# Last layer of a four-layer convolution kernel: loads and stores cut into parts, and border transfers issued by ScalarE instead of SyncE

## The chip, the cores and the metric

The program runs on one core of one Trainium2 chip. The metric is the device time of one execution, in microseconds (us). The core has five engines that run beside each other, each through its own list of instructions in order: TensorE (PE in the profile, its weight loads PEld), VectorE (DVE), ScalarE (ACT), GpSimd (POOL) and SyncE (SP). They meet only at semaphores. DMA transfers are issued by an engine's instruction list and then run beside it; SP and ACT have a queue of their own each.

## The reference

Four layers, each of which adds a residual. Only the last is touched by the change. Its core, on x of 4 images x 48 channels x 256 x 256 in float32:

```
x = x + _L3_conv_ref(_gn(x), w_in, w_dw, fft_mask, w_out)

y = jnp.einsum('oc,bchw->bohw', w_in, x)                  # 48 -> 288 channels
f = jnp.fft.rfft2(yp) * fft_mask[None]                    # on patches of 8 x 8
yp = jnp.fft.irfft2(f, s=(P, P))
y = lax.conv_general_dilated(y, w_dw, (1, 1), ((1, 1), (1, 1)), feature_group_count=C2)   # 3 x 3, each channel alone
x1, x2 = jnp.split(y, 2, axis=1)
g = jax.nn.gelu(x1, approximate=False) * x2
return jnp.einsum('oc,bchw->bohw', w_out, g)              # 144 -> 48 channels
```

## The kernel before

The last layer is `stage_l3`. It is unrolled: 66 **slabs**, n = 0 to 65. A slab is a band of 8 image rows (33 bands, of which the last only closes the image) of two images at once; patches are 8 x 8 = 64 pixels, 32 patches to a band. The filter with the mask and the 3 x 3 convolution are folded into one matrix for each channel, `d` (64 x 100: a patch of 8 x 8 in, 10 x 10 out). The ring of one pixel around each patch belongs to its neighbours and has to be added there: left and right by a transfer from partition to partition (`edge`), below through a saved strip (`strip`).

What PE does in a slab, in this order (`slab` at L2348; the line of the matmul in brackets):

- `convolve(n, 0)` (L2298): 5 groups of channels from `y` and `d` into PSUM banks
- `transpose(n-1, 2)` (L2320): the gated result of the slab before, channel block 2, turned
- `convolve(n, 1)` (L2298), then `project(n-1)` (L2334), the last matmul of the slab before
- `transpose(n, 0)` (L2320), which waits for both halves of the gated block 0 of this slab
- `convolve(n, 2)` (L2298)
- `channels(n+1)` (L2255): the 1 x 1 matmul of the next slab, in 12 groups, from `x` to PSUM
- `transpose(n, 1)` (L2320)

Each convolved **block** (j = 0, 1, 2; u = 3n + j counts all of them) goes the same way. ACT copies one half of each PSUM bank pair to `turn` (L2389, called from `read_turn`) and DVE the other (L2383). When both are through (`a_out`, `b_out`), POOL sets a border to zero (L2523, it then signals `parted`), and two DMAs carry the outer columns of `turn` to `edge`, one for each side (L2203, in `move_edges`; 126 partitions of 1920 bytes). The second waits for `parted`. POOL then zeroes the ends of `edge` (L2526), adds `edge` (L2528), adds `strip` (L2534, in every band but the first; it signals `carried`) and saves the new strip (L2538, it signals `saved`, without which the next block's L2523 doesn't start). ACT computes the Gelu of two halves (L2396, it waits for `carried`), DVE multiplies each half with its gate (L2472), PE transposes, and ACT copies the turned banks to `rows` (`read_rows`, L2389). After `project`, DVE adds the residual in four pieces m (L2480, `f_out`), and the slab is stored.

What sets the order of the transfers is SP's list (`slab` at L2226), which holds every transfer of the layer. For slab n:

- `load_x(n+1)` when `channels(n)` has read the last of `x` (there is one `x` buffer): for each of two images 48 partitions x 8 KB in one DMA (L2187), and a row of ones on one partition (L2189)
- `move_edges(n, 0)` and `move_edges(n, 1)`
- `store(n-1)`: two DMAs of 384 KB (L2209), when all four pieces of the result are there
- `move_edges(n, 2)`
- `load_residual(n)`: four DMAs of 192 KB (L2218), when the store has landed

ACT's own list before the change (`slab` at L2411): the five copies of block 0 with the two Gelu halves of the slab before between them; four `read_rows` copies of `transpose(n-1, 2)`; the five copies of block 1; the two Gelu halves of block 0; four `read_rows` copies; the five copies of block 2; then the 12 copies of `channels(n+1)` (`read_y`) with the two Gelu halves of block 1 between them; and four `read_rows` copies. `conv_at(n, j, g)` is the count at which group g of block j of slab n begins in `a_done` (PE has written) and `a_out` (ACT has read).

Of the kernel before, what the change touches and what calls it, by code (L numbers as in the profile page):

```python
# [16 lines left out]
B, C, H, W = 4, 48, 256, 256  # L17
# [5 lines left out]
HI = 64  # L23
# [2072 lines left out]
def stage_l3(nc, D, S):  # L2096

    C3 = 3 * C
    TX, PX = W // 8, 64
    BANDS = H // 8 + 1  # L2100
    N = 2 * BANDS
# [9 lines left out]
    LANE = 32  # L2111
    GROUPS = PX // 4
    with nc.cleanup_on_exit(), ExitStack() as ctx:
        def sb(name, shape):
# [5 lines left out]
        def sem(name):  # L2120
            return nc.alloc_semaphore(f"l3_{name}")
# [20 lines left out]
        d_in = [sem(f"d_in{j}") for j in range(3)]  # L2142
        x_loaded, res_loaded, stored = sem("x_loaded"), sem("res_loaded"), sem("stored")
        edge_in = [sem("edge_in0"), sem("edge_in1")]
# [7 lines left out]
        def conv_at(n, j, g):  # L2152

            return n * AB + YR + j * COMP + g
# [21 lines left out]
        def _(sp):  # L2176
            for dst, src in ((win, "l3_win"), (wout[:], "l3_wout")):
                sp.dma_start(dst, D[src]).then_inc(consts, 16)

            def load_x(q, ty, n, first):  # L2180
                if not first:
                    sp.wait_ge(a_done, n * AB - (AB - YR))
                    sp.wait_ge(b_done, n * AB - (AB - YR))
                for s in range(2):
                    at = B * NBLK if ty == BANDS - 1 else ty + (q + 2 * s) * NBLK
                    src = D["x3p"][bass.ds(at + 2, 1)]
                    sp.dma_start(x[s * HI:s * HI + C].rearrange("p t x -> p (t x)"), src.rearrange("a c n -> (a c) n"))\  # L2187
                      .then_inc(x_loaded, 16)
                    sp.dma_start(x[s * HI + C:s * HI + C + 1].rearrange("p t x -> p (t x)"), D["k_ones3"][bass.ds(ty, 1), :])\  # L2189
                      .then_inc(x_loaded, 16)  # L2190

            def move_edges(n, j):

                u = n * 3 + j
                sp.wait_ge(a_out, conv_at(n, j, COMP))
                sp.wait_ge(b_out, conv_at(n, j, COMP))
                if u >= 2:
                    sp.wait_ge(edged, u - 1)
                here, there = slice(0, 126), slice(2, 128)
                for side, column, dst, src in ((0, 9, there, here), (1, 0, here, there)):  # L2200
                    if side == 1:
                        sp.wait_ge(parted, u + 1)
                    sp.dma_start(edge[dst, u % 2, side, :],  # L2203
                                 turn[src, u % 2, column].rearrange("p y g i -> p (y g i)")).then_inc(edge_in[u % 2], 16)

            def store(n):
                sp.wait_ge(f_out, n * 4 + 4)
# [4 lines left out]
            def load_residual(q, ty, n, first):  # L2212
                if not first:
                    sp.wait_ge(stored, n * 32)
                for s in range(2):
                    for side in range(2):
                        src = D["x3"][q + 2 * s, :, ty * 8 + 4 * side:ty * 8 + 4 * side + 4, 1:W + 1]
                        sp.dma_start(out[side * HI:side * HI + C, :, s, :], src).then_inc(res_loaded, 16)  # L2218
            load_x(0, 0, 0, True)
            for j in range(3):  # L2220
# [15 lines left out]
            store(N - 1)  # L2236
            sp.wait_ge(stored, N * 32)

        @block.tensor
        def _(pe):  # L2240
            def channels(q, n, first):

                pe.wait_ge(x_loaded, n * 64 + 64)
                for g, size in enumerate(SIZES):
# [142 lines left out]
        def _(act):  # L2387
# [3 lines left out]
            def gelu(u, h):  # L2391
# [198 lines left out]
```

## Time and profile before

| | us |
|---|---|
| median of 3 runs | 12194.6 (12163.93 to 12206.02) |
| the profiled execution | 12186.19 |
| its span on the core | 12184.1 |
| of it the last layer, about | 9442 to 12153 |

The page of the profile gives the busy time of each engine, a strip of 40 slices of the span, the queues of the DMA engines, and the groups of instructions with what ended the idle time before them. The releaser "issue" stands for time in which an engine waited for nothing that the profile shows. The rows are taken from one execution. In the rows names of buffers stand without their prefix and number: l_x is `x`, l_turn is `turn`, l_a, l_b and l_e are the PSUM banks. q1 is SP's queue, q8 and q14 are queues of kind "instruction".

### The profile page before, as it was taken

What the parts mean: (1) busy time and instruction counts of PE and PEld (TensorE: products, weight loads), DVE (VectorE), ACT (ScalarE), POOL (GpSimd) and SP (SyncE); (2) the same over time, 40 slices, a digit from 0 to 9 for tenths busy, and PEclk for the clock granted to TensorE, in tenths of its full rate; (3) what the DMA queues carried; (4) which work ended last, traced back from release to release, by engine and by line L of the source; (5) the groups of instructions that cost most, each with busy time, mean ns of one, the idle gap of its engine ahead of it and who ended that gap; (6) DMA issues with size and microseconds to landing.
All of it is one profiled execution on the core that took longest, in us unless ns stands there. A gap on an engine that the chain in (4) does not pass through costs nothing. (4 is left out here: it accounts for less than half of the span.)

```text
span 12184.1 us, 377334 instructions
## 1 busy us (share of the span) xinstructions
PE 11485.7 (94%) x157286; PEld 8059.9 (66%) x157286; DVE 7073.4 (58%) x16108; ACT 5169.6 (42%) x10670; POOL 4924.0 (40%) x4166
## 2 busy tenths in 40 slices
PE   8999999899979999899999999999999888888888
PEld 7877444399977777555555555555555777777776
DVE  0000355544435544688888888888887665566655
ACT  0000111143433333355555555555554666666666
POOL 0000222211430045566666666666665444444444
PEclk9999999999989999899999999999999999999999
DMA  4333466695894489766666666666665443344433
GB/s 141 132 131 133 126 159 157 151 169 102 149 169 150 135 211 231 115 88 88 88 88 89 88 88 89 88 88 88 88 88 78 109 101 92 92 100 96 99 91 91
DMA packets 2340706, 1418.36 MB, mean 116 GB/s; under 512 B 1877404, under 2 KB 2250395, under 8 KB 2253487
## 3 DMA queue, kind: packets, MB, share of 16 engines
q1 hardware_dynamic: 2064428, 1296.69, 53.7%
q10 hardware_dynamic: 275072, 105.14, 3.7%
q8 instruction: 812, 13.30, 0.5%
q14 instruction: 394, 3.23, 0.1%
HBM read 648.90 MB, written 450.45 MB: 90 GB/s over the span
## 5 line engine op out<-in xcount | busy, mean ns | idle before, releaser
L1795 PE MATMUL l_m<-l_wa,l_pix 128*128 128x288 f32 x8192 | 2210.6, 413 | 2.7 <-DVE l_wb L1977 2.7
L1795 PEld LDWEIGHTS l_m<-l_wa,l_pix 128*128 128x128 f32 x8192 | 1475.1, 190 | 688.4 <-issue 361.5
L1651 POOL TENSOR_TENSOR l_qkv<-l_qkv,l_copies 128x576 f32<-128x576 f32 x1024 | 1437.0, 1403 | 629.2 <-DVE l_qkv L1988 618.4
L1641 POOL TENSOR_TENSOR l_pix<-l_raw 128x516 f32<-128x516 f32 x1024 | 1217.1, 1189 | 1043.5 <-DVE l_t L2025 1018.2
L1476 PE MATMUL l1h_ps<-l1h_ring,l1h_w 96*96 96x256 f32 x6120 | 1327.2, 379 | 63.6 <-ACT l1h_ring L1418 60.0
L1476 PEld LDWEIGHTS l1h_ps<-l1h_ring,l1h_w 96*96 96x96 f32 x6120 | 999.1, 163 | 391.6 <-issue 60.2
L1509 DVE SCALAR_TENSOR_TENSOR l1h_ring<-l1h_ps,l1h_bias,l1h_columns 96x256 f32<-96x256 f32 x1020 | 671.1, 658 | 677.3 <-PE l1h_ps L1476 671.6
L509 PE MATMUL l0a_rows<-l0a_x 128*49 128x245 f32 x8144 | 1043.8, 371 | 0.0
L870 PE MATMUL l0b_bank<-l0b_x,l0b_w 49*64 49x512 f32 x9216 | 1001.1, 593 | 4.4 <-DVE l0b_w L896 4.4
L1890 ACT ACTIVATE l_ks<-l_f 94x384 f32<-94x384 f32 x1024 | 498.7, 487 | 838.6 <-PE l_f L1810 838.6
L1810 PE MATMUL l_f<-l_qkv,l_a 64*94 64x384 f32 x4096 | 835.0, 483 | 1.6 <-POOL l_qkv L1651 1.5
L870 PEld LDWEIGHTS l0b_bank<-l0b_x,l0b_w 49*64 49x64 f32 x9216 | 438.8, 133 | 563.9 <-issue 563.9
L1801 PE MATMUL l_m<-l_wb,l_left 58*128 58x288 f32 x4096 | 773.9, 455 | 0.0
L1460 POOL TENSOR_TENSOR l1h_columns<-l1h_blocks,l1h_ring 96x2048 f32<-96x2048 f32 x63 | 351.0, 5595 | 1035.0 <-DVE l1h_ring L1509 1035.0
L1901 ACT ACTIVATE l_y<-l_i,l_shift,l_rsd 128x96 f32<-128x96 f32 x2048 | 711.2, 428 | 14.3 <-DVE l_shift L2015 0.6
L1895 ACT ACTIVATE l_sd<-l_mv,l_eps 128x4 f32<-128x4 f32 x512 | 152.2, 297 | 1288.0 <-DVE l_mv L2008 1288.0
L1224 PE MATMUL l1v_ps<-l1v_ring_w,l1v_w 48*48 48x130 f32 x20480 | 633.3, 273 | 45.9 <-ACT l1v_ring_w L1147 39.1
L509 PEld LDWEIGHTS l0a_rows<-l0a_x 128*49 128x49 f32 x8144 | 601.4, 124 | 107.7 <-issue 1.4
L2383 DVE COPY l_turn<-l_b 128x500 f32<-128x500 f32 (+1 forms) x528 | 351.6, 666 | 471.8 <-PE l_b L2298 471.5
L2298 PE MATMUL l_e<-l_d,l_y 64*64 64x100 f32 x17424 | 497.0, 255 | 134.5 <-issue 128.4
L1224 PE MATMUL l1v_ps<-l1v_ring_p,l1v_w 48*48 48x128 f32 x20320 | 616.0, 269 | 5.3 <-issue 4.9
L1224 PEld LDWEIGHTS l1v_ps<-l1v_ring_w,l1v_w 48*48 48x48 f32 x20480 | 588.0, 120 | 49.0 <-issue 48.8
(272 smaller groups left out, 22221.3 us busy)
## 6 DMA issues: line engine op xcount, KB each, us to landing
l0a_x<-x_px_dram SPq DMA_DIRECT2D x128, 1176.0 KB, 5.1
l_edge<-l_turn SPq DMA_DIRECT2D x396, 236.2 KB
l0b_x<-x_in_dram SPq DMA_DIRECT2D x128, 493.8 KB
l_raw<-l_raw SPq DMA_DIRECT2D x128, 483.6 KB, 7.3
l_raw<-x_dram SPq DMA_DIRECT2D x1270, 48.0 KB, 3.6
l_x<-x3p_dram SPq DMA_DIRECT2D x132, 384.0 KB
l_out<-x_dram SPq DMA_DIRECT2D x264, 192.0 KB, 4.4
out_dram<-l_out SPq DMA_DIRECT2D x132, 384.0 KB, 4.5
```

What stands on the lines that cost most here:

```text
L509: last = nc.tensor.matmul(o[odd * ODD:odd * ODD + C1, lo:lo + n * C1], x[:, ks, ys, 2 + odd, :], x[:, k, y, e0 + odd:e0 + odd + n, :].rear ...
L870: last = nc.tensor.matmul(bank[2 * n + rt][h * HI:(h + 1) * HI, :], w[part, t, :], rows(part, k, 4 * n + h + t // 3 - rt)[:, :, t % 3:t % ...
L1224: last = nc.tensor.matmul(ps[g][side(c), r, 0:width], w[side(r), t, :], x, start=(t == 0), stop=(t == TAPS - 1), skip_group_check=True)
L1476: last = nc.tensor.matmul(ps[g][0:C2, 0:GI * V], w[:, kernel, s, :], ring[:, g, before % DEEP, :, s:s + V], start=(s == 0), stop=(s == 2))
L1509: nc.vector.scalar_tensor_tensor(out=ring[:, g, x % DEEP, :, 1:V + 1], in0=ps[g][0:C2, 0:GI * V].rearrange("p (i v) -> p i v", i=GI), scal ...
L1641: nc.gpsimd.tensor_tensor(pix[:, n % 2, i, half * HALF:(half + 1) * HALF].rearrange("p (r w) -> p r w", w=PW), in0, in1, op).then_inc(pix_ ...
L1651: nc.gpsimd.tensor_tensor(q, q, copies[:, g % 2, 1:2, :].broadcast_to([128, 2, OUTC]), ALU.add)\
L1795: last = nc.tensor.matmul(bank[i][:, 0:OUTC], pix[:, k, i, first:first + 128], wa[:, b, i, :], start=True, stop=(i in (1, 2)))
L1801: nc.tensor.matmul(bank[i][:, 0:OUTC], left[rows, k, first:first + 128], wb[rows, b, :], start=False, stop=True).then_inc(conv_done, 1)
L1810: last = nc.tensor.matmul(f[0:SLOTS, h, 0:2 * QK].rearrange("p (n o) -> p n o", n=2), a[k, 0:SLOTS], qkv[k, j % 4, 2 * r:2 * r + 2, 0:QK], ...
L1890: nc.scalar.activation(ks[:, r % 2], f[0:SLOTS, :, 0:2 * QK].rearrange("p h (n o) -> p h n o", n=2)[:, :, :, C2:QK], ACT.Copy).then_inc(k_ ...
L1901: last = nc.scalar.activation(y[:, g, m, :], iv[:, m * C2:(m + 1) * C2], ACT.Identity, scale=rsd[:, g, m:m + 1], bias=shift[:, g, m:m + 1])
```

## The change

All in `stage_l3`:

- **x** is loaded in four parts of 8 patches for each image (48 x 2 KB, 96 KB): the first when `channels(n)` is through, the others behind group 2 of `convolve(n, 0)` and groups 0 and 2 of `convolve(n, 1)`. The row of ones is loaded for 4 of the 66 slabs only (where its content changes).
- **The store** is cut into the four pieces m for each of two sides (96 KB), each when DVE has added its residual and PE has come to group m of `convolve(n, 2)`.
- **The residual load** keeps its four DMAs; they are spread over groups 2, 5, 8 and 11 of `channels(n+1)`.
- **The border transfers** leave SP. ACT issues them on its own queue, each pair behind ACT's last copy of the block, with the same waits.

```diff
-            def load_x(q, ty, n, first):
-                if not first:
-                    sp.wait_ge(a_done, n * AB - (AB - YR))
-                    sp.wait_ge(b_done, n * AB - (AB - YR))
+            def load_x(n, k):
+
+                ty, q = n % BANDS, n // BANDS
+                tiles = slice(k * TX // PARTS, (k + 1) * TX // PARTS)
                 for s in range(2):
                     at = B * NBLK if ty == BANDS - 1 else ty + (q + 2 * s) * NBLK
-                    src = D["x3p"][bass.ds(at + 2, 1)]
-                    sp.dma_start(x[s * HI:s * HI + C].rearrange("p t x -> p (t x)"), src.rearrange("a c n -> (a c) n"))\
-                      .then_inc(x_loaded, 16)
+                    src = D["x3p"][at + 2].rearrange("c (t x) -> c t x", x=PX)
+                    sp.dma_start(x[s * HI:s * HI + C, tiles], src[:, tiles]).then_inc(x_loaded, 16)
...
+            def store(n, m):
+                sp.wait_ge(f_out, n * 4 + m + 1)
                 for side in range(2):
-                    sp.dma_start(D["out"][n, side], out[side * HI:side * HI + C].rearrange("p y s w -> p (y s w)"))\
-                      .then_inc(stored, 16)
...
+                    sp.dma_start(D["out"][n, side].rearrange("c (y n) -> c y n", y=4)[:, m],
+                                 out[side * HI:side * HI + C, m].rearrange("p s w -> p (s w)")).then_inc(stored, 16)
...
             def slab(q, ty, n, first, last):
                 if not last:
-                    load_x(*((1, 0) if q == 0 and ty == BANDS - 1 else (q, ty + 1)), n + 1, False)
-                move_edges(n, 0)
-                move_edges(n, 1)
+                    sp.wait_ge(a_done, n * AB + YR)
+                    sp.wait_ge(b_done, n * AB + YR)
+                    if n + 1 in ONES:
+                        load_ones(n + 1)
+                    load_x(n + 1, 0)
+                    sp.wait_ge(a_done, conv_at(n, 0, 3))
+                    load_x(n + 1, 1)
+                if not last:
+                    for k in range(2, PARTS):
+                        sp.wait_ge(a_done, conv_at(n, 1, 2 * k - 3))
+                        load_x(n + 1, k)
+                for m in range(4):
+                    if not first:
+                        if m > 0:
+                            sp.wait_ge(a_done, conv_at(n, 2, m))
+                        store(n - 1, m)
                 if not first:
-                    store(n - 1)
-                move_edges(n, 2)
-                load_residual(q, ty, n, first)
+                    sp.wait_ge(stored, n * 128)
+                for k in range(4):
+                    if not last:
+                        sp.wait_ge(a_done, (n + 1) * AB + 3 * k + 2)
+                    load_residual(q, ty, k // 2, k % 2)
...
+            def move_edges(n, j):
+
+                u = n * 3 + j
+                act.wait_ge(a_out, conv_at(n, j, COMP))
+                act.wait_ge(b_out, conv_at(n, j, COMP))
+                if u >= 2:
+                    act.wait_ge(edged, u - 1)
+                here, there = slice(0, 126), slice(2, 128)
+                for side, column, dst, src in ((0, 9, there, here), (1, 0, here, there)):
+                    if side == 1:
+                        act.wait_ge(parted, u + 1)
+                    nc.scalar.dma_start(edge[dst, u % 2, side, :],
+                                 turn[src, u % 2, column].rearrange("p y g i -> p (y g i)")).then_inc(edge_in[u % 2], 16)
...
                     read_turn(act, copy, 0, n, 0, g, a_done, a_out)
                     if g in (0, 2) and not first:
                         gelu(u - 1, g // 2)
+                move_edges(n, 0)
                 if not first:
                     read_rows(n - 1, 2)
                 for g in range(COMP):
                     read_turn(act, copy, 0, n, 1, g, a_done, a_out)
+                move_edges(n, 1)
                 for h in range(2):
                     gelu(u, h)
                 read_rows(n, 0)
                 for g in range(COMP):
                     read_turn(act, copy, 0, n, 2, g, a_done, a_out)
+                move_edges(n, 2)
```

On ACT, from the last copy of block 0 to the Gelu of block 0. Before:

```order
L2389 ACTIVATE l_turn<-l_e 128x100x4
L2389 ACTIVATE l_rows<-l_a 128x512
L2389 ACTIVATE l_rows<-l_b 128x512
L2389 ACTIVATE l_rows<-l_e 128x512 x2
L2389 ACTIVATE l_turn<-l_a 128x100x5
L2389 ACTIVATE l_turn<-l_e 128x100x5
L2389 ACTIVATE l_turn<-l_a 128x100x5 x2
L2389 ACTIVATE l_turn<-l_a 128x100x4
L2396 ACTIVATE l_turn<-l_turn 128x8x4x24 x2
```

and in the changed kernel, in which L2397 is the copy, L2404 the Gelu and L2417 the border transfer:

```order
L2397 ACTIVATE l_turn<-l_e 128x100x4
L2417 DMA l_edge<-l_turn 126x480 x2
L2397 ACTIVATE l_rows<-l_a 128x512
L2397 ACTIVATE l_rows<-l_b 128x512
L2397 ACTIVATE l_rows<-l_e 128x512 x2
L2397 ACTIVATE l_turn<-l_a 128x100x5
L2397 ACTIVATE l_turn<-l_e 128x100x5
L2397 ACTIVATE l_turn<-l_a 128x100x5 x2
L2397 ACTIVATE l_turn<-l_a 128x100x4
L2417 DMA l_edge<-l_turn 126x480 x2
L2404 ACTIVATE l_turn<-l_turn 128x8x4x24 x2
```

The pair of block 0 now stands ahead of the four copies to `rows`, and the pair of block 1 ahead of the Gelu of block 0.

On SP, one slab before (l_x from x3p is the load of x, l_out from x_dram the residual, out_dram the store):

```order
L2187 DMA l_x<-x3p_dram 48x2048
L2189 DMA l_x<-k_ones_dram 1x2048
L2203 DMA l_edge<-l_turn 126x480 x4
L2209 DMA out_dram<-l_out 48x2048 x2
L2203 DMA l_edge<-l_turn 126x480 x2
L2218 DMA l_out<-x_dram 48x4x256 x4
```

(the first two rows stand there twice in turn), and in the changed kernel:

```order
L2189 DMA l_x<-x3p_dram 48x512 x8
L2201 DMA out_dram<-l_out 48x512 x8
L2207 DMA l_out<-x_dram 48x4x256 x4
```

The border transfers and, in most slabs, the ones are gone from SP's list; x and the store go out in eight DMAs each.

## Rows read from the trace of the kernel before

**Rows 1.** The page, queues of the DMA engines: packets, MB, share of 16 engines.

```profile
q8 instruction: 812, 13.30, 0.5%
```

**Rows 2.** Busy by stretch: PE, PEld, DVE, ACT, POOL, clock, DMA share, GB/s.

```profile
9442.00:12153.00 2711.00, 2323.68 (x64288) 1948.03 (x64288) 1652.97 (x2435) 1760.79 (x2959) 1186.72 (x978) 0.95 0.40 97
```

**Rows 3.** Waits of PE in the last layer: us in total, times, longest.

```profile
PE l_e L2298 <- issue: 128.4, 55, 5.0
PE l_e L2255 <- issue: 50.3, 47, 3.3
PE l_a L2255 <- issue: 41.7, 36, 3.3
PE l_a L2320 <- DVE l_gate L2472: 39.7, 39, 6.4
PE l_a L2298 <- issue: 34.3, 21, 3.3
PE l_b L2255 <- issue: 30.6, 20, 3.2
PE l_b L2298 <- issue: 28.9, 20, 3.4
```

**Rows 4.** The chain that ended last, one slab: start us, us, what.

```profile
9734.48 2.58 issue
...
9740.13 0.80 SPq L2203
...
9740.98 3.42 DMA l_edge<-l_turn
...
9759.84 1.01 issue
...
9764.99 0.75 issue
```

**Rows 5.** DMA queues from 9731.4 to 9734.1, behind the load of x: packets, MB, share.

```profile
q1 hardware_dynamic: 70, 0.40, 92.1%
```

**Rows 6.** The same from 9734.1 to 9736: packets, MB, share.

```profile
q1 hardware_dynamic: 16, 0.02, 8.0%
q8 instruction: 1, 0.02, 5.4%
```

**Rows 7.** The same from 9740 to 9744, two border transfers in flight.

```profile
q1 hardware_dynamic: 278, 0.48, 37.7%
q8 instruction: 1, 0.02, 1.5%
```

**Rows 8.** SP's DMA issues in the slab, in order of time: start us, us.

```profile
9728.98 0.31 SPq L2187 DMA_DIRECT2D l_x<-x3p_dram  x1
...
9754.36 0.79 SPq L2209 DMA_DIRECT2D out_dram<-l_out  x2
...
9761.25 2.02 SPq L2218 DMA_DIRECT2D l_out<-x_dram  x4
```

**Rows 9.** The border transfers' issue on SP, ns min/median/max.

```profile
L2203 SPq DMA_DIRECT2D l_edge<-l_turn x396: 759/782/1756, 9462.5 to 12155.0; - x198
```

**Rows 10.** POOL in the slab, in order of time: start us, us [idle before].

```profile
9749.31 0.82 POOL L2538 COPY l_strip<-l_turn 128x768 f32<-128x768 f32 x1 [0.17 <-POOL l_turn L2534]
9750.37 0.49 POOL L2523 MEMSET l_turn<- 2x480 f32 x1 [0.24 <-POOL l_strip L2538]
```

**Rows 11.** ACT, DVE and PE at the Gelu of block 0, each engine's order of time.

```profile
9749.24 1.58 ACT L2396 ACTIVATE l_turn<-l_turn 128x768 f32<-128x768 f32 x2 [3.32 <-POOL l_turn L2534]
...
9750.11 1.83 DVE L2472 TENSOR_TENSOR l_gate<-l_turn 128x768 f32<-128x768 f32 x2 [4.08 <-ACT l_turn L2396]
...
9751.22 0.63 PE L2320 MATMUL l_a<-k_ident,l_gate 128*128 128x128 f32 x4 [0.53 <-DVE l_gate L2472]
```

**Rows 12.** ACT from block 0's last copy: start us, us, in order of time.

```profile
9739.28 0.60 ACT L2389 ACTIVATE l_rows<-l_a 128x512 f32<-128x512 f32 x1
...
9758.71 0.72 ACT L2389 ACTIVATE l_y<-l_e 128x432 f32<-128x432 f32 x1 [0.28 <-PE l_e L2255]
```

More of the change, by code:

```diff
@@ L2112, in stage_l3 @@
     GROUPS = PX // 4
+    PARTS = 4
+    ONES = (0, BANDS - 1, BANDS, N - 1)
     with nc.cleanup_on_exit(), ExitStack() as ctx:
@@ L2142, in stage_l3 @@
         d_in = [sem(f"d_in{j}") for j in range(3)]
-        x_loaded, res_loaded, stored = sem("x_loaded"), sem("res_loaded"), sem("stored")
+        x_loaded, res_loaded, stored, ones_in = sem("x_loaded"), sem("res_loaded"), sem("stored"), sem("ones_in")
         edge_in = [sem("edge_in0"), sem("edge_in1")]
@@ L2178, in _ @@
                 sp.dma_start(dst, D[src]).then_inc(consts, 16)
-            def load_x(q, ty, n, first):
-                if not first:
-                    sp.wait_ge(a_done, n * AB - (AB - YR))
-                    sp.wait_ge(b_done, n * AB - (AB - YR))
+            def load_x(n, k):
+                ty, q = n % BANDS, n // BANDS
+                tiles = slice(k * TX // PARTS, (k + 1) * TX // PARTS)
                 for s in range(2):
                     at = B * NBLK if ty == BANDS - 1 else ty + (q + 2 * s) * NBLK
-                    src = D["x3p"][bass.ds(at + 2, 1)]
-                    sp.dma_start(x[s * HI:s * HI + C].rearrange("p t x -> p (t x)"), src.rearrange("a c n -> (a c) n"))\
-                      .then_inc(x_loaded, 16)
-                    sp.dma_start(x[s * HI + C:s * HI + C + 1].rearrange("p t x -> p (t x)"), D["k_ones3"][bass.ds(ty, 1), :])\
-                      .then_inc(x_loaded, 16)
@@ L2192, in move_edges @@
[L2192 to L2204, printed above, removed]
@@ L2206, in store @@
-            def store(n):
-                sp.wait_ge(f_out, n * 4 + 4)
-                for side in range(2):
-                    sp.dma_start(D["out"][n, side], out[side * HI:side * HI + C].rearrange("p y s w -> p (y s w)"))\
-                      .then_inc(stored, 16)
[L2212 to L2218, printed above, removed]
@@ L2219, in _, with load_ones @@
-            load_x(0, 0, 0, True)
+                    src = D["x3p"][at + 2].rearrange("c (t x) -> c t x", x=PX)
+                    sp.dma_start(x[s * HI:s * HI + C, tiles], src[:, tiles]).then_inc(x_loaded, 16)
+            def load_ones(n):
+                ty = n % BANDS
+                for s in range(2):
+                    sp.dma_start(x[s * HI + C:s * HI + C + 1].rearrange("p t x -> p (t x)"), D["k_ones3"][bass.ds(ty, 1), :])\
+                      .then_inc(ones_in, 16)
+            def store(n, m):
+                sp.wait_ge(f_out, n * 4 + m + 1)
+                for side in range(2):
+                    sp.dma_start(D["out"][n, side].rearrange("c (y n) -> c y n", y=4)[:, m],
+                                 out[side * HI:side * HI + C, m].rearrange("p s w -> p (s w)")).then_inc(stored, 16)
@@ L2220, in _, with load_residual @@
+            def load_residual(q, ty, s, side):
+                src = D["x3"][q + 2 * s, :, ty * 8 + 4 * side:ty * 8 + 4 * side + 4, 1:W + 1]
+                sp.dma_start(out[side * HI:side * HI + C, :, s, :], src).then_inc(res_loaded, 16)
+            load_ones(0)
+            for k in range(PARTS):
+                load_x(0, k)
             for j in range(3):
@@ L2227, in slab @@
                 if not last:
-                    load_x(*((1, 0) if q == 0 and ty == BANDS - 1 else (q, ty + 1)), n + 1, False)
-                move_edges(n, 0)
-                move_edges(n, 1)
-                if not first:
-                    store(n - 1)
-                move_edges(n, 2)
-                load_residual(q, ty, n, first)
+                    sp.wait_ge(a_done, n * AB + YR)
[14 more added lines that the diff above has]
+                        store(n - 1, m)
+                if not first:
+                    sp.wait_ge(stored, n * 128)
[3 more added lines that the diff above has]
+                    load_residual(q, ty, k // 2, k % 2)
             slabs(slab)
-            store(N - 1)
-            sp.wait_ge(stored, N * 32)
+            for m in range(4):
+                store(N - 1, m)
+            sp.wait_ge(stored, N * 128)
         @block.tensor
@@ L2241, in channels @@
             def channels(q, n, first):
-                pe.wait_ge(x_loaded, n * 64 + 64)
+                pe.wait_ge(x_loaded, (n + 1) * 2 * PARTS * 16)
+                pe.wait_ge(ones_in, 32 * len([k for k in ONES if k <= n]))
                 for g, size in enumerate(SIZES):
```

## Prediction

> **What bounds the kernel now.** The change touches the last layer alone, so I read that stretch, some 2711 us with 66 slabs, 41.1 us each. PE is busy for 2324 of them, DVE 1653, ACT 1761, POOL 1187 [rows 2]: PE sets the pace, and 387 us are its gaps. The list of PE's waits splits them. The largest are put down to "issue", that is, to nothing that the profile knows: ahead of L2298 (the convolutions) 128.4 + 34.3 + 28.9 = 191.6 us in 96 gaps, ahead of L2255 (the 1 x 1 matmul) 50.3 + 41.7 + 30.6 = 122.6 us in 103 gaps. The next is DVE's gate (L2472), 39.7 us in 39 waits [rows 3]. So 314 us, or 4.8 us of a slab, have no named cause.
>
> I take one slab apart. PE stops for 2.58 us at 9734.48, in `convolve(n, 0)`, for 1.01 us at 9759.84 and for 0.75 us at 9764.99, both in `channels` [rows 4]. What runs then? The program fetches its instructions by DMA: 812 packets on q8, 13.30 MB, so 16 KB each [rows 1]. SP issued the load of x at 9728.98 [rows 8]. From 9731.4 to 9734.1 its packets hold 92.1% of the DMA engines and there is no packet of q8 [rows 5]; q8's packet falls in the next window, when SP's queue has 0.02 MB left [rows 6], and PE goes on at 9737.06. A fetch of instructions that is asked for while x is loading therefore comes after it. The two gaps in `channels` lie in the same way behind the store (issued at 9754.36) and in the residual load (from 9761.25) [rows 4, 8]. Against that, while two border transfers are in flight (0.48 MB, 37.7%), a fetch comes through and PE has no gap [rows 7]. I read the 314 us as late fetches behind large transfers.
>
> Second, a chain that PE hardly shows: PE's transpose of block 0 at 9751.22 waits 0.53 us for the gate [rows 11]. The chain of waits leads from there back over DVE, ACT's Gelu and POOL to the border transfer of block 0, 3.42 us of flight, and to its issue at 9740.13 [rows 4]. 39 of 66 slabs end `project` in such a wait [rows 3]. For those slabs anything added between the border transfer and the gate is added to the slab.
>
> **The load of x in four parts.** The volume in flight behind `channels` falls from 768 KB to 192 KB, and two 8 KB rows of ones go. Now 0.40 MB take 2.7 us [rows 5], so 0.2 MB take about 1.3 us; issued at the same place, they are through at the time that the fetch is asked for, or a microsecond behind it. I put what is left of the gap in `convolve(n, 0)` at 0.4 us. The other parts are issued some 3 to 5 us apart, which is more than they take. The gaps ahead of L2298 are 191.6 / 66 = 2.9 us a slab. Gain: 2.2 us, between 1.5 and 2.5.
>
> **Store and residual.** The residual's four DMAs go out over all of `channels` in place of 2.02 us [rows 8]. The store's pieces are held back only by groups 1 to 3 of `convolve(n, 2)`, so that much of it stays one burst, though the last piece is issued a little later than the whole was. The gaps ahead of L2255 are 122.6 / 66 = 1.9 us a slab. I take a gain of 1.2, between 0.4 and 1.8. At the end of the program only 192 KB stand behind the last piece: 2 us once. Four more issues of x and six of the store on SP cost nothing, since SP has only transfers left and waits for PE between them.
>
> **The border transfers on ACT.** This is the cost. An issue takes SP's list 0.78 us [rows 9]; no row shows it on ACT, and I take the same, from 0.3 (what the load of x takes on SP) to 1.2.
>
> Block 0: ACT copies to `rows` from 9739.28 [rows 12]. It would now wait for DVE's last copy, to 9740.13 (SP's issue, which has the same wait [rows 4]), and issue twice: 9741.8. The four copies to `rows` and, behind them, the copies of block 1 start up to 2.5 us late, and PE waits for these banks inside `convolve(n, 1)`. That would delay `project` by at most 2.5 us.
>
> Block 1: its second transfer waits for `parted`, and on ACT this now stands ahead of the Gelu of block 0. POOL gives it after `saved`: the strip copy from 9749.31 and the memset from 9750.37 to 9750.86 [rows 10]. The Gelu started at 9749.24 [rows 11]. Now it starts after 9750.86 + 0.03 + 0.78 + 0.04 = 9751.71: 2.5 us later (2.0 to 2.9 over the bounds of the issue). DVE's gate behind it and PE's transpose, which starts 0.15 us after the first gate half has ended, move by the same 2.5 us. This runs beside the delay of `project` from block 0, so the larger of the two counts and not the sum. PE already waits in 39 slabs; in the others it comes later than the gate, on the mean by some 0.3 us over all, which is slack: 2.2 us. Then parts 3 and 4 of x are issued in `convolve(n, 1)`, beside the border transfer of block 0, and 0.2 MB more at the rate of [rows 5] may lengthen its flight: 0.4 us, 0 to 1.0. Together a cost of 2.6 us, 1.9 to 3.3.
>
> Block 2: ACT's first copy of `channels` at 9758.71 [rows 12] comes about 1.6 us later. PE runs four groups ahead of it there, and ACT's busy share is 1761 / 2711 = 65% [rows 2], so it catches up: nothing, or up to 0.3 us if it doesn't.
>
> What SP gains from the removal is worth nothing: a wait of SP for the border is no longer ahead of other transfers, but x was loaded ahead of it anyway. The Trainium skill's page "DMA: Bandwidth & Descriptors", section "Issuing engines are not separate DMA queues", speaks against this part of the change too: starting DMAs from several engines saves only the sequencer's time to start them. By it the transfer's flight wouldn't shorten; the sum above has no gain for it either way.
>
> **The sum.** -2.2 - 1.2 + 2.6 = -0.8 us a slab, x 66 = -53 us, and -2 us at the end. From the profiled execution's 12186 us that is 12131. The median of the runs lies 8 us above that execution, which is within their spread (12164 to 12206); I add half of it: 12135 us.
>
> **Rivals.**
>
> *The chain doesn't take it.* The border transfers leave SP's queue and might land earlier, and an issue on ACT might be short. Of 3.42 us of flight [rows 4] perhaps 1 us goes, the issue costs 0.3, and the cost is 1.2 us a slab. With gains of 2.4 and 1.5: -2.7 x 66 = -178 us, 12010 us. For it: ACT stands idle for 3.32 us ahead of the Gelu [rows 11]. Against: all this idle time is before `carried`, and the wait for `parted` comes after it. Chance 0.14.
>
> *ACT becomes the bound* (slower than before). If the delays of block 0 and of the chain add up, since `project` starts late and its own DVE and ACT work then comes on top, or if an issue on ACT takes 1.2 us, the cost is 2.6 + 1.6 = 4.2 us. With gains of 2.0 and 0.8 the net is +1.4 x 66 = +92 us, 12278 us. It decides where the cost passes the gain of 3.4 us a slab. For it: six more issues, 4.7 us a slab, on an engine at 65% which stands between PE's banks. Chance 0.18.
>
> *The late fetches aren't due to the size of the transfers.* Then the gaps stay, and only the cost is left: +2.6 x 66 = +172 us, 12358 us. For it: one window can't tell a fetch asked for late from one served late. Against: the gaps fall behind the load of x, and a burst of another kind left PE alone [rows 5 to 7]. Two sections of the Trainium skill would have it so. "Runtime: NRT & Kernel Launch", section "Instruction fetch mechanics", calls the crossing of a 16 KiB block mostly hidden; the trace disagrees, with 4.8 us a slab [rows 3]. "DMA: Bandwidth & Descriptors", section "Queues, rings and completion order", has each DMA engine take turns between queues packet by packet, so that a fetch would wait for one packet and not for all of x; the window without q8 speaks against it [rows 5]. Chance 0.06.
>
> *The parts do nothing in effect:* smaller transfers, now spread over the whole slab, meet every fetch and delay each a little, so that half of the gaps stay. Gains 1.4 and 0.8, cost 2.3: about 0, 12190 us. Chance 0.12.
>
> My forecast, from -0.3 to -1.7 us a slab, has 0.50.
>
> **The numbers.** A run of this kernel can tell about 0.3%, 37 us, from no change. Faster by more than that: the first rival (0.14), most of the forecast (0.43) and 0.03 of the fourth rival, 0.60. Within it: 0.07 of the forecast, 0.06 of the fourth, 0.01 of the second, 0.14. Slower: 0.17 of the second, the third (0.06) and 0.03 of the fourth, 0.26. The range that leaves out 2 in 10 goes from 12030 to 12285; it leaves out the third rival and the better half of the first.
>
> **What would show it.** Right: in `convolve(n, 0)` the "issue" gaps of 2 to 3 us fall below 0.5 us, and the sum ahead of L2298 from 191.6 to under 60 us; PE's wait for DVE's gate rises from 39.7 us to 100 us and more, in nearly all slabs; ACT's Gelu is released by its own border transfer or POOL's memset. Wrong: the gaps ahead of L2298 stay over 120 us (then fetches are late for another reason); PE's wait for the gate stays (then the issue is cheap or the flight shorter); waits of PE for ACT's copies in `convolve(n, 1)` or in `channels` of over 1 us a slab (then ACT bounds).

## The result and the profile after

The changed kernel takes 12247.4 us (median of 6 runs, 12242.6 to 12253.3) against 12191.8 us of 6 runs of the kernel before: a ratio of 1.0048, with a 95% interval of 1.0035 to 1.0061. It is slower by 56 us where 57 us less were forecast. The profiled execution took 12242.6 us, its span is 12240.7.

Its last layer runs from about 9442 to 12208, 55 us longer than before. Busy time by stretch, in the columns of [rows 2] with their header. The first row is the whole layer, and the others are the end of a `project`, the wait behind it, the transposes of block 0 and the start of `convolve(n, 2)` in one slab of the changed kernel:

```profile
core 0: us, PE busy (x) PEld busy (x) DVE busy (x) ACT busy (x) POOL busy (x), PEclk, DMA share, GB/s
9442.00:12208.00 2766.00, 2350.45 (x64288) 1937.73 (x64288) 1633.91 (x2434) 1680.11 (x2958) 1187.44 (x979) 0.95 0.34 95
9771.00:9776.30 5.30, 5.30 (x100) 1.83 (x96) 0.57 (x1) 0.51 (x1) 4.81 (x4) 1.00 0.15 49
9776.40:9779.20 2.80, 0.00 (x0) 0.00 (x0) 1.07 (x2) 1.58 (x2) 0.00 (x0) 1.00 0.27 86
9779.20:9782.00 2.80, 2.77 (x20) 2.46 (x21) 2.80 (x5) 1.69 (x3) 2.48 (x2) 0.67 0.17 46
9782.00:9783.50 1.50, 1.50 (x38) 1.50 (x41) 0.35 (x1) 0.60 (x1) 1.42 (x2) 0.50 0.22 56
```

PE's waits in the layer, which answer to [rows 3]: us in total, times, longest (L2306 is the convolution, L2263 the 1 x 1 matmul, L2328 the transpose, L2497 the gate):

```profile
PE l_a L2328 <- DVE l_gate L2497: 204.6, 68, 10.4
PE l_e L2306 <- issue: 29.5, 42, 2.6
...
PE l_a L2306 <- ACT l_turn L2397: 28.2, 64, 0.5
PE l_e L2263 <- issue: 24.7, 32, 2.4
PE l_a L2306 <- ACT l_rows L2397: 22.7, 61, 1.1
...
PE l_a L2263 <- issue: 11.3, 13, 2.2
PE l_e L2328 <- DVE l_gate L2497: 11.0, 18, 4.4
...
PE l_a L2306 <- issue: 8.6, 13, 1.6
...
PE l_b L2263 <- issue: 5.8, 10, 1.2
PE l_b L2306 <- issue: 4.6, 7, 1.4
```

That these gaps are fetches of instructions shows in the trace of before. Of its 123 "issue" gaps over 1 us ahead of these two matmuls, 121 lie whole multiples of 256 instructions apart in PE's own list, and 117 end 1.2 to 1.6 us after a 16 KB packet of q8 has ended. Of PE's 18 other gaps over 1 us none is at such a place, and 2 end so.

The late fetches went as forecast: ahead of the convolutions 29.5 + 8.6 + 4.6 = 42.7 us are left of 191.6, ahead of the 1 x 1 matmul 24.7 + 11.3 + 5.8 = 41.8 of 122.6 [rows 3]. That is 229.7 us less. Against it stand the gate, 204.6 us in place of 39.7, and waits for ACT's copies (28.2 + 22.7) that weren't there. In all, PE's idle time in the layer went from 387 us (2711 - 2324) to 416 (2766 - 2350). The chain of waits of the same slab shows where the gate's time is made. The columns are those of [rows 4]:

```profile
9764.74 0.78 ACTq L2417
...
9765.56 4.31 DMA l_edge<-l_turn
...
9772.79 1.83 POOL l_turn L2559
...
9774.78 0.83 POOL l_strip L2563
...
9775.84 0.50 POOL l_turn L2548
9776.37 0.78 ACTq L2417
...
9777.25 0.85 ACT l_turn L2404
...
9779.23 0.63 PE l_a L2328 x4
9779.86 0.45 PE l_b L2328 x4
9780.31 0.85 PE l_a L2328 x4
9781.16 0.85 PE l_b L2328 x4
```

POOL is through with what the Gelu needs at 9774.62. But ACT's next instruction is the second border transfer of block 1, which waits for POOL's strip copy and memset, and the Gelu starts at 9777.25, 2.6 us later; before, it started 0.1 us after POOL's add [rows 11]. And there is something that I hadn't forecast at the end of the same rows. Of the 16 transposes behind the wait the third group of four takes 0.85 us and the fourth as well, where the second takes 0.45. The granted clock, 1.00 in the stretch without work, is 0.67 on the mean of this one, and in the next it is 0.50, the lower of its two levels (1.2 GHz in place of 2.4), though PE is busy for all of it.

So that the parts can be compared, I divide a slab at the first matmul of each phase and take the mean distance over the 64 inner slabs of each trace, in us. T stands for `transpose`, "to T(n,0)" is T(n-1,2), `convolve(n, 1)` and `project` together:

| | channels | T(n,1) | conv 0 | to T(n,0) | T(n,0) | conv 2 | slab |
|---|---|---|---|---|---|---|---|
| before | 11.67 | 2.05 | 7.73 | 13.02 | 1.98 | 4.66 | 41.12 |
| changed | 10.65 | 2.03 | 5.17 | 16.33 | 2.96 | 4.71 | 41.85 |

`channels` and `convolve(n, 0)` give 3.6 us, the way to T(n,0) takes 3.3 more and the transposes take 1.0 more.

### The profile page after: what moved, and what is told of

Its sections match the earlier page's. It is cut to its first block and busy times, and to the rows that moved or that the text cites. A ratio compares the mean times of both kernels' runs of the same rounds, so it can differ in the third digit from the quotient of the medians.

```text
span 12240.7 us, 378261 instructions
## 1 busy us (share of the span) xinstructions
PE 11514.5 (94%) x157286; PEld 8061.5 (66%) x157286; DVE 7057.6 (58%) x16108; ACT 5092.6 (42%) x10670; POOL 4928.7 (40%) x4166
## 5 line engine op out<-in xcount | busy, mean ns | idle before, releaser
L2497 DVE TENSOR_TENSOR l_gate<-l_turn 128x768 f32<-128x768 f32 x396 | 432.5, 1106 | 462.9 <-ACT l_turn L2404 462.7
```

Source lines behind the costliest of these rows:

```text
L2497: nc.vector.tensor_tensor(gated_half(u, h), half(u, 0, h), half(u, 1, h), ALU.mult).then_inc(gate_out, 1)
```

## The experiments

Each ran beside the kernel before on the same chip. The medians of before differ by 0.2% from one such group of runs to another (12166 to 12192), so the ratio counts; differences in us between two kernels of different groups are good to some 25 us. Sums from PE's list of waits, in us: "conv" and "1 x 1" are the issue gaps ahead of these matmuls, "gate" the two rows of waits for L2472, or its line there.

| kernel | us | ratio (95%) | conv | 1 x 1 | gate |
|---|---|---|---|---|---|
| before | 12192 | | 191.6 | 122.6 | 42.8 |
| changed | 12247 | 1.0048 (1.0035, 1.0061) | 42.7 | 41.8 | 215.6 |
| e1: all parts, borders on SP | 11962 | 0.9828 (0.9809, 0.9848) | 52.4 | 37.3 | 76.9 |
| e2: borders on ACT alone | 12460 | 1.0237 (1.0209, 1.0266) | 161.5 | 159.9 | 159.9 |
| e3: changed, pair behind the Gelu | 12027 | 0.9890 (0.9871, 0.9909) | 37.7 | 29.3 | 46.7 |
| e4: ones seldom alone | 12197 | 1.0021 (1.0009, 1.0033) | 186.7 | 117.6 | 43.0 |
| e5: x in parts alone | 12034 | 0.9875 (0.9858, 0.9891) | 60.4 | 110.9 | 71.7 |
| e6: store and residual alone | 12133 | 0.9960 (0.9943, 0.9976) | 217.4 | 41.2 | 42.9 |
| e7: e1 with two parts of x | 11958 | 0.9812 (0.9795, 0.9828) | 87.3 | 43.4 | 49.0 |
| e8: e1, parts 3 and 4 in project | 11942 | 0.9804 (0.9788, 0.9821) | 56.6 | 39.0 | 56.8 |
| e9: changed, wait filled | 12179 | 0.9993 (0.9982, 1.0005) | 47.2 | 35.0 | 54.3 |
| e10: changed, parts 3 and 4 in project | 12186 | 0.9999 (0.9984, 1.0013) | 40.1 | 33.2 | 180.5 |
| e11: e8, DVE's last copy first | 11919 | 0.9776 (0.9758, 0.9793) | 64.7 | 37.2 | 64.6 |

Beside these columns stands one more row of issue gaps, ahead of the transposes of block 1, behind `channels` (l_e): 6.5 us before, 21.5 in the changed kernel, 47.3 in e1, 27.4 in e6 and 38.0 in e11, with 2.2 us at the most for one. So a part of what the fetches gave comes back in that place. But these gaps aren't fetches: the rows under e1 show what PE waits for there.

### e1: the border transfers back on SP

```diff
 # SP, slab n of the changed kernel
+                move_edges(n, 0)
                 if not last:
                     for k in range(2, PARTS):
                         sp.wait_ge(a_done, conv_at(n, 1, 2 * k - 3))
                         load_x(n + 1, k)
+                move_edges(n, 1)
                 for m in range(4):
...
                         store(n - 1, m)
+                move_edges(n, 2)
 # ACT
-                move_edges(n, 0)
-                move_edges(n, 1)
-                move_edges(n, 2)
```

> The changed kernel with the border transfers back on SP, each pair at the place in SP's list where it is due (block 0 ahead of x parts 3 and 4, block 1 ahead of the stores, block 2 ahead of the residual). Theory (two effects that add up: the parts end the late fetches, ACT's list costs): PE's issue gaps stay where the changed kernel has them, near 85 us in place of 314, and the wait for the gate goes back to some 40 us; 12190 - 200 = 11990 us, 11950 to 12030. Rival A (the fetches came in time only because ACT held PE back and gave them time): the issue gaps return to over 200 us and the time is near 12190. Rival B (the parts of x beside the border transfer lengthen its flight, whoever issues it): the wait for the gate stays over 100 us, 12080 or more.

PE's waits of e1 (L2323 the convolution, L2280 the 1 x 1 matmul, L2345 the transpose):

```profile
PE l_a L2345 <- DVE l_gate L2497: 64.3, 58, 6.7
PE l_e L2345 <- issue: 47.3, 30, 2.1
PE l_e L2323 <- issue: 32.9, 43, 3.7
PE l_e L2280 <- issue: 22.5, 41, 1.5
...
PE l_e L2345 <- DVE l_gate L2497: 12.6, 28, 2.9
PE l_a L2323 <- issue: 10.6, 17, 1.8
PE l_b L2323 <- issue: 8.9, 14, 1.0
```

The gaps of the second row lie ahead of the transposes of block 1. The profile names no releaser, but each of the 28 of them over 0.7 us ends 0.10 us after DVE's copy of one of the last banks of `channels`, and their places in PE's list don't repeat every 256 instructions. One of them, from 9759.32 to 9760.92 (start us, us; L2398 is DVE's copy, L2553 POOL's add of `edge`):

```profile
9757.40 2.24 POOL L2553 TENSOR_TENSOR l_turn<-l_turn,l_edge 128x960 f32<-128x960 f32 x1
9758.12 2.33 DVE L2497 TENSOR_TENSOR l_gate<-l_turn 128x768 f32<-128x768 f32 x1
9760.37 0.45 DVE L2398 COPY l_y<-l_e 128x288 f32<-128x288 f32 x1
9760.92 0.45 PE L2345 MATMUL l_e<-k_ident,l_gate 128*128 128x128 f32 x1 [1.60 <-issue]
```

The copy is late because the gate ahead of it took 2.33 us. A gate half with no copy or add of POOL beside it takes 0.95 us (the mean of 261 in e1); 56 of the 396 take over 1.5 us, all beside POOL's adds, and each of the 30 gaps of this row follows one. No run here tests this cause by taking POOL's work away.

11962 us, 1.7% faster than before. The fetches come in time without ACT holding PE back, so rival A falls. The way to T(n,0) takes 13.60 us against 13.02 before, not 16.33: rival B falls as the main cause, though 0.6 us of it is real, and the wait for the gate stays above its 40 us (76.9 by both rows).

### e2: the border transfers on ACT, nothing else

```diff
 # kernel before
 # SP
-                move_edges(n, 0)
-                move_edges(n, 1)
-                move_edges(n, 2)
 # ACT, behind its last copy of each block
+                move_edges(n, 0)
+                move_edges(n, 1)
+                move_edges(n, 2)
```

> The kernel before with the border transfers alone moved to ACT; loads and stores as before. Theory (the effects add up): issue gaps near 314 us as before, wait for the gate near 200 us as in the changed kernel; 12247 + 230 = 12480 us, 12400 to 12520. Rival A (an ACT that holds PE back gives the fetches time, so that the gaps shrink by themselves): issue gaps under 200 us, 12300 to 12380. Rival C (the border transfers out of SP's queue already shorten the wait of the fetches): the gaps ahead of the 1 x 1 matmul fall below 60 us from 123.

12460 us, 2.4% slower. Its gaps in the same list (L2281 convolution, L2238 the 1 x 1 matmul, L2303 transpose):

```profile
PE l_a L2303 <- DVE l_gate L2472: 150.9, 69, 7.0
PE l_e L2281 <- issue: 106.2, 50, 4.7
PE l_e L2238 <- issue: 74.1, 38, 4.6
```

The gaps stay at 161.5 + 159.9 = 321 us in all, against 314 before. So the border transfers' move doesn't help the fetches, and rivals A and C both fall. The two parts of the change add up nearly: -1.7% (e1) and +2.4% (e2) make +0.65%, the change has +0.48%.

### e3: block 1's pair behind the Gelu of block 0

```diff
                 for g in range(COMP):
                     read_turn(act, copy, 0, n, 1, g, a_done, a_out)
-                move_edges(n, 1)
                 for h in range(2):
                     gelu(u, h)
+                move_edges(n, 1)
                 read_rows(n, 0)
```

> The changed kernel with one move on ACT: the pair of border transfers of block 1 stands behind the two Gelu halves of block 0 and no longer ahead of them. Theory (the wait for parted ahead of the Gelu is the cost): Gelu starts 2.5 us earlier, PE's wait for the gate falls from 205 us to under 70, the transposes of block 0 run at the full clock again (2.0 us in place of 3.0); 12247 - 66 x 3 = 12050 us, 12000 to 12100. Rival D (the cost is the late issue and longer flight of block 0's pair, and ACT's copies behind it): under 60 us come back, 12190 or more.

This one line gives back 220 us (193 by the ratios; 3.4 us x 66 = 223 by the mean slab, 38.47 us against 41.85): 12027 us. PE's waits:

```profile
PE l_e L2263 <- ACT l_y L2397: 42.2, 52, 1.5
PE l_e L2328 <- ACT l_y L2397: 35.8, 48, 1.4
...
PE l_a L2328 <- DVE l_gate L2497: 32.5, 41, 7.2
```

The gate's wait is down to 32.5 us, the way to T(n,0) to 13.81 us, and the transposes take 1.96 us again. Rival D is out. What is left against e1, some 65 us, lies where PE waits for ACT's copies in and behind `channels` (42.2 and 35.8 us): `channels` takes 11.03 us against 10.30 in e1. There the pair of block 2, for which I had set nothing or at the most 0.3 us, costs up to 0.7 us a slab, or the copies that come later since the pair of block 1 now stands ahead of `read_rows`; no run tells these two apart.

### e4: the row of ones in 4 slabs only

```diff
                       .then_inc(x_loaded, 16)
+                    if n in ONES:
                         sp.dma_start(x[s * HI + C:s * HI + C + 1]...
```

> The kernel before with one thing of the change: the row of ones is loaded in 4 of the 66 slabs. Theory (volume in flight is what delays a fetch): 16 of 784 KB go, so at most 20 us: 12170 to 12195, gaps ahead of the convolutions near 190 us as before. Rival E (the rows on one partition, 8 KB each on a single DMA engine, are what the fetch waits behind, and not the volume): the gaps ahead of the convolutions fall from 192 us below 110, 12110 or less.

No gain: gaps of 186.7 us ahead of the convolutions against 191.6, time 0.2% above before. That the fetch sits behind the rows of ones is out. Why it is even a little slower, 1.0009 at the least, stays open; 0.2% is also what before's own median moves from group to group.

### e5 and e6: x alone, store and residual alone

e5 has `load_x` in four parts, with `store`, `load_residual` and their waits as before; e6 has these two from the change and `load_x` as before. The border transfers are on SP in both.

> The kernel before with the load of x in four parts and seldom ones, the border transfers on SP; store and residual load as before. Theory (each burst delays the fetches behind it alone): the issue gaps ahead of the convolutions fall from 192 us to under 70, those ahead of the 1 x 1 matmul stay near 120; some 150 us less gaps, and up to 40 us back through the border transfer of block 0, beside which parts 3 and 4 run: 12050, 12010 to 12090 us. Rival (a backlog over the whole slab delays the fetches): both groups of gaps fall by a similar share, each by less than half.

> The kernel before with the store in four pieces and the residual load spread over the 1 x 1 matmul; x in one go, the border transfers on SP. Theory: the issue gaps ahead of the 1 x 1 matmul fall from 123 us to under 60, those ahead of the convolutions stay near 190; 12190 - 75 = 12110, 12080 to 12150 us. With the run of x in parts alone it adds up to the 205 us of the run with all parts on SP. Rival: the store's pieces are the same burst as before, and the gaps stay over 90 us.

PE's waits in e5 (L2317 the convolution, L2274 the 1 x 1 matmul):

```profile
PE l_e L2274 <- issue: 48.8, 47, 3.3
PE l_a L2274 <- issue: 38.1, 32, 3.3
PE l_e L2317 <- issue: 37.8, 38, 3.9
```

and in e6 (L2304, L2261):

```profile
PE l_e L2304 <- issue: 140.7, 53, 5.3
...
PE l_e L2261 <- issue: 23.9, 41, 1.5
```

Each transfer delays the fetches that are asked for behind it, and no others: x in parts brings the gaps ahead of the convolutions from 192 to 60 us and leaves the others (111), the store and residual bring those of the 1 x 1 matmul from 123 to 41 and leave the first (217, even a little more). The gains are 1.25% and 0.40%, together 1.65% against 1.72% for both in e1. The rivals, a backlog over the whole slab and a store that stays a burst, are out. e6 gains about 49 us (0.0040 x 12192), though its gaps ahead of the 1 x 1 matmul are 81 us fewer: 26 us come back ahead of the convolutions, where x is loaded in one go, and 21 ahead of the transposes of block 1, where PE waits for DVE.

### e7: two parts of x in place of four

```diff
-    PARTS = 4
+    PARTS = 2
```

> All loads and stores spread and the border transfers on SP (the run that took 11962 us), with x in two parts of 384 KB in place of four of 192. Theory (what is in flight when the fetch is asked for delays it): a gap of about 1.2 us comes back in convolve(n, 0), the gaps ahead of the convolutions rise from 52 us to 100 to 140; 12010, 11985 to 12040 us. Rival (any cut is enough, since the fetch needs a break between two DMAs): within 10 us of 11962.

The time is the rival's, 11958 us, but its reason isn't. With 384 KB in flight the gaps ahead of the convolutions do rise, from 52.4 to 87.3 us, less than the 100 that I had set as the least. What makes up for it is that no part of x is issued any more in `convolve(n, 1)`, beside block 0's border transfer: the way to T(n,0) is 13.33 us in place of 13.60. `convolve(n, 0)` is 0.5 us longer (5.58 against 5.07), the way to T(n,0) 0.3 shorter and T(n,1) 0.15: small effects against each other.

### e8: parts 3 and 4 of x behind convolve(n, 1)

```diff
-                        sp.wait_ge(a_done, conv_at(n, 1, 2 * k - 3))
+                        sp.wait_ge(a_done, conv_at(n, 1, COMP))
```

> All loads and stores spread and the border transfers on SP, with parts 3 and 4 of x issued when convolve(n, 1) is through and no longer inside it. Theory (these parts run beside block 0's border transfer and lengthen its flight, and PE waits for that chain in 58 slabs): the flight shortens by 0.5 to 0.8 us, PE's wait for the gate falls from 64 us to under 45; 11925, 11900 to 11945 us. Rival (the chain ends later only because convolve(n, 0) is shorter and DVE is behind it): the same time within 10 us.

11942 us, 20 us less than e1, but the times alone don't show it: the intervals of 0.9804 and 0.9828 overlap, and so do the runs (11935 to 11953 against 11947 to 11974). The rows do. The border transfer of block 0 lands, on the mean, 6.37 us behind the start of T(n-1,2) in place of 6.76, and the way to T(n,0) falls from 13.60 to 13.23 us. So the flight shortened by 0.4 us, where 0.5 at the least was expected, and the wait for the gate fell from 64.3 to 46.7 us in its first row, a little less than forecast.

### e9: the wait filled with work

```diff
+                    if j == 0 and i == 0:
+                        for fill in range(20):
+                            nc.tensor.transpose(bank[:, (fill % 4) * 128:(fill % 4 + 1) * 128], S["k_ident"][:],
+                                                S["k_ident"][:])
                     if i % 2 == 0:
                         pe.wait_ge(gate_out, u * 2 + 1 + i // 2)
```

> The changed kernel with 20 more transposes of a constant ahead of PE's wait for the gate of block 0 (their result is overwritten by the real ones, nothing else changes), some 2.4 us of work in a wait of 2.9. Theory (after an idle PE the clock falls, and the transposes of block 0 take 3.0 us in place of 2.0 for that alone): they take 2.0 us again, PEclk behind the wait is 1.0, and 66 us come back less what the filling costs where the wait was shorter: 12190, 12170 to 12215 us. Rival (these transposes wait for the second gate half or for something else of ACT's and DVE's): they still take 3.0 us, and the time is 12247 or more.

The kernel does more work and is faster than the changed one by 69 us: 12179 us. Busy time by stretch, in one slab of e9, first the filling and then the 16 transposes:

```profile
9562.30:9564.60 2.30, 2.30 (x22) 2.17 (x20) 0.93 (x2) 1.58 (x2) 0.00 (x0) 1.00 0.33 105
9564.60:9566.70 2.10, 2.10 (x18) 1.72 (x16) 2.10 (x5) 1.27 (x3) 1.69 (x2) 1.00 0.00 0
```

PEclk stays at 1.00 and the transposes take 2.1 us (from 9564.68 to 9566.75). Over the 64 inner slabs they take 2.06 us at a granted clock of 1.00, against 2.96 us at 0.66 in the changed kernel and 1.98 at 0.99 before. So 0.9 of the microsecond that they had lost is the clock's, granted low after PE had stood idle for 2.9 us, and not a wait for the second gate half: 59 of the 69 us. The way to T(n,0) is 0.16 us shorter too, which makes the rest.

### e10: the changed kernel with parts 3 and 4 of x in project

The edit is that of e8, made in the changed kernel, with the border transfers on ACT.

> The changed kernel, the border transfers on ACT, with parts 3 and 4 of x issued when convolve(n, 1) is through. Theory (the parts lengthen block 0's flight here too, by what they did with the transfers on SP): 20 us less, 12210 to 12240. Rival (ACT's queue takes turns with SP's, so that the parts don't matter): 12247 as it is, within 8 us.

12186 us, 61 us less, three times what I had set. Block 0's border transfer lands 0.57 us earlier (6.46 us behind T(n-1,2) in place of 7.03), which makes 38 us. With it PE's wait is shorter (168.8 us at the gate in place of 204.6), and T(n,0) takes 2.77 us in place of 2.96, which makes 13 us more. Some 10 of the 61 us stay unexplained, within what two groups of runs differ by. The two queues don't shield a transfer on one from the traffic of the other. The Trainium skill says so too, on the page "DMA: Bandwidth & Descriptors", section "Issuing engines are not separate DMA queues"; the trace agrees, with these 0.57 us.

### e11: DVE's last copy of block 0 ahead of its second gate half

```diff
 # DVE, in e8
-                    if g in (1, 3) and not first:
-                        gated(u - 1, g // 2)
+                    if g in (1, 4) and not first:
+                        gated(u - 1, g // 4)
```

> The fastest kernel so far (11942 us: all loads and stores spread, parts 3 and 4 of x behind convolve(n, 1), the border transfers on SP) with one swap on DVE: its last copy of block 0 comes ahead of the second gate half of the block before, and no longer behind it. Theory (PE still ends project in a wait for the chain that begins with DVE's last copy of block 0): block 0's border transfer is issued up to 0.9 us earlier, PE's wait for the gate at project's end falls from 47 us to under 30, and up to 0.3 us a slab is lost at the transposes of block 2, whose gate comes later; 11910, 11885 to 11930 us. Rival (PE is bound by its own work by now): 11942 or a few us more.

PE's waits for the gate in e11:

```profile
PE l_e L2345 <- DVE l_gate L2497: 48.4, 66, 2.4
...
PE l_a L2345 <- DVE l_gate L2497: 16.2, 8, 8.8
```

11919 us, 2.2% faster than before and the fastest of all. The wait at the end of `project` (l_a) is down from 46.7 us in 48 slabs to 16.2 in 8, and the price is the wait at the transposes of block 2 (l_e), 48.4 us, as expected. With that the chain from block 0's border transfer bounds PE no longer at the end of `project` in most slabs. The interval (0.9758 to 0.9793) still touches that of e8 (0.9788 to 0.9821).

## Why the prediction was wrong, point by point

**The late fetches: right.** The gain ahead of the convolutions was set at 2.2 us a slab and is (191.6 - 42.7) / 66 = 2.3; ahead of the 1 x 1 matmul it was set at 1.2 and is (122.6 - 41.8) / 66 = 1.2. e5 and e6 show each with its own cause. The rival that the size of the transfers doesn't matter is out. Of the two rules of the Trainium skill that were set beside it, the first doesn't hold for this kernel. That the crossing of a block is mostly hidden ("Runtime: NRT & Kernel Launch", section "Instruction fetch mechanics"): 314 us of gaps, spaced by 256 instructions, speak against it. The second isn't settled. That the queues take turns packet by packet ("DMA: Bandwidth & Descriptors", section "Queues, rings and completion order"): if a fetch waited for one small packet, cutting x into parts would have brought little, and it brought 1.25% (e5). But the same section of the Trainium skill counts some 9 to 17 descriptors to a packet, and the trace has 96 records of 8 KB for the two DMAs of x, 6 for each of 16 engines, so that a whole load could be one such turn. No run here tells. (The prediction reads the fetch's late start from one window; it doesn't show when the fetch was asked for.)

**The wait ahead of the Gelu: right in kind and size.** I had 2.5 us from POOL's strip copy, its memset and one issue on ACT. The rows show an issue of 0.78 us on ACT, just as on SP, and a Gelu 2.6 us behind POOL's add in place of 0.1. e3, which moves this pair alone, gives back 220 us.

**Its cost on PE's path: too low.** The step that failed is "Together a cost of 2.6 us, 1.9 to 3.3": the change costs 4.3 us a slab at this place. 0.7 of the missing 1.7 us lie in the terms that it adds up, 1.0 in a term that it doesn't have, the clock. First the terms. The way to T(n,0) grew by 3.31 us. Two terms of it were too small. The flight beside parts 3 and 4 of x was set at 0.4 us; the landing is 7.03 us behind T(n-1,2) in place of 5.95, of which 0.35 us are the later release and 0.73 the flight. And the release itself I had left where it was: with `convolve(n, 0)` 2.6 us shorter, DVE's copies and gates there no longer hide in PE's gap, and POOL's memset, which follows DVE's last copy, comes at 1.65 us behind T(n-1,2) in place of 1.30. It is the shorter `convolve(n, 0)` and not ACT's part that does this: 1.71 us in e5, which has only x in parts, and 1.34 in e2, which has only the transfers on ACT. A gap that goes takes its cover with it. (The Gelu's delay, 2.6 us, and the slack of 0.3 us that goes off it were as I had them.)

**What wasn't in the sum at all: the clock.** This is the larger part of the miss. A wait of 2.9 us at one place of every slab costs more than its length, since the transposes behind it ran in part at the lower level: T(n,0) took 2.96 us in place of 1.98. e9 shows the cause. 1.0 us x 66 = 65 us is more than the whole difference between before and after. Over the whole layer the mean granted clock is 0.95 on both sides ([rows 2] and the first row above), but its low stretches moved. Means over the 64 inner slabs: `channels` went from 0.95 to 1.00, `convolve(n, 0)` from 0.94 to 1.00 and T(n-1,2) from 0.90 to 1.00, where the fetch gaps went; T(n,0) fell from 0.99 to 0.66 and `convolve(n, 2)` from 1.00 to 0.92, behind the new wait. I had priced the clock on neither side.

With the measured terms the sum is -2.3 - 1.2 + 3.3 + 1.0 = +0.8 us a slab, +53 us in all, against 56 measured. It closes in part because two things that it leaves out nearly cancel: PE's busy time in `channels` and `convolve(n, 0)` fell by 0.95 us a slab too, at the higher clock, and idle time of about that size came in there, 0.55 us of it at DVE's and ACT's copies in and behind `channels`. By the table of distances the slab is 0.73 us longer, 48 us in all.

**The rivals.** The one that ends slower named a cost of 4.2 us and 12278 us; the cost is 4.3, and the time 12247. Its price was right by luck, since its mechanism was wrong: the delay of block 0's copies and that of the chain didn't add up (PE waited 0.15 us behind the gate in all 64 slabs, and for nothing else there), and an issue on ACT didn't take 1.2 us. PE's waits for ACT's copies came to 0.8 us a slab in `convolve(n, 1)` and 0.5 in and behind `channels`, each below the 1 us that was to show ACT as the bound. The first rival, a border transfer that lands earlier on its own queue, is out by e2, where it lands at 5.94 us, as before (5.95). I had given 0.60 to faster for gains that were right, and had taken the cost from the exposed wait alone.

**The range** held the time only because it was wide; the forecast in its middle had the wrong sign.

## What to carry to other kernels

A wait that is moved to another engine stands ahead of all that is queued there: the transfer was harmless on SP, which has nothing else to do, and cost 220 us on ACT because the Gelu that PE's chain hangs on stood behind it. Large loads that go out in one burst can starve the fetch of instructions of an engine with a long unrolled list; cut them to parts and spread them, and keep the parts away from a small transfer that a chain waits for. Where a change shortens one engine's gap, look at who else worked in that gap, and count a long idle of PE with the slow matmuls behind it.

## What the runs showed of the hardware that I hadn't expected

- PE stood idle for 2.8 us (busy 0.00, PEclk 1.00), and the low level came only behind that, in the midst of work: the second four of the transposes took 0.45 us, the last two fours 0.85 us each, and the stretch after them was at 0.50. Filling the wait with useless transposes kept it at 1.00 and made the kernel 69 us faster (e9).
- Late fetches of instructions cost PE some 314 us in this layer before the change, all put down to "issue" by the profile. They are told from other waits by their places, 256 instructions apart, and by the packet of q8 that ended 1.2 to 1.6 us earlier. Not every "issue" gap is one: those ahead of the transposes of block 1 (47.3 us in e1) were waits for DVE.
- DVE's gate half took 0.95 us alone and up to 2.97 us beside POOL's adds (e1).
- A 126-partition border transfer takes 0.78 us to issue on ACT, the same as on SP (0.78), and its landing isn't earlier from ACT's own queue: 5.94 us behind T(n-1,2) in e2 against 5.95 before. With parts 3 and 4 of x beside it, it is even later from ACT (7.03 us, against 6.76 from SP in e1, with the same issue time); why stays open.
